# Attention's weights times values: values as the streaming operand from rows of 272 bytes, and first values loaded ahead of the second queries

## The chip, the cores and the metric

The kernel runs on one core of one Trainium2 chip. The metric is the device time of one execution in microseconds (us). Three runs of the kernel before took 785.93, 788.27 and 789.87 us, median 788.27. Engine names: PE is TensorE, DVE is VectorE, ACT is ScalarE, POOL is GpSimd, SP is the engine whose queue issues nearly all transfers.

## The reference

`x` has shape (4, 512, 512), 2048 tokens of 512 features. Attention here is across heads within a token: every token has 32 heads of 16 features, and its 32x32 scores compare its own heads.

```python
q = (x @ wq.T + bq).reshape(B, S, 32, 16)      # k and v alike
scores = einsum('bshd,bstd->bsht', q, k) / sqrt(16)
context = einsum('bsht,bstd->bshd', softmax(scores), v).reshape(B, S, 512)
x = layernorm(x + context)
dq1, dq2, dq3 = nf4_quant_dequant(w1), ...     # 15 comparisons per element, blocks of 64
h = silu(x @ dq1.T) * (x @ dq2.T)              # 1376 hidden features
x = layernorm(x + h @ dq3.T)
```

## The kernel before

The program is written engine by engine, each with its own order of instructions, joined by semaphores. It has three stages.

**Projections.** 48 steps (`tau`), 12 for each of 4 blocks of 512 tokens, make queries, keys and values. They are stored to `qk_parts` and `v_blocks` in HBM and loaded back in the layout of the attention.

**Attention.** It works on 8 half blocks of 256 tokens (`hb`). A half block holds 4 sets `q` of 64 tokens, and 4 groups. So there are 32 groups `G`, each of 16 positions times 4 sets, that is 64 tokens. In each group:

- `scores` (PE): 64 matmuls of 32x32 into `ps_s`.
- `highest`, `shift` (DVE): the row maximum and its subtraction, `prob`; `exp` (ACT); `swap` (DVE): a 32x32 block transpose into `probT`, done one group later.
- `values` (PE), two groups later: for each of the 16 positions the values `v_bd[:, :, position]` are the stationary operand and `probT` the streaming one. `v_bd` is block diagonal over the four sets, 128 partitions by 68 columns (4 sets of 16 features and a column of ones) by 64 positions. Columns of one position stand 64 floats, 256 bytes, apart. The result in `ps_p` has 68 partitions and 32 columns a position.
- `context` (ACT): copies the group's 68x512 from PSUM to `ctx`, three groups later.

After 8 groups (a block of 512 tokens) five `ct` turns transpose `ctx` back to tokens and `add_context` (DVE) divides by the sum and adds to `part`; then `moments`, `norm_1` (ACT, 4 instructions), and four `xt` turns transpose the normalised tokens for the FFN. For the first three blocks this happens inside the groups of the next block: `ct` in groups 8b+10 to 8b+12, moments in 8b+12, norm in 8b+13, `xt` in 8b+14 and 8b+15.

**FFN.** 44 steps of gate, up and down matmuls.

Between all this runs the quantisation of the weights: 15 levels for each of 28 units, one `steep` on ACT and one `lift` on DVE for a level (`nf_y`, `nf_acc`). `LV_A` says how many levels a group takes: 2, and 1 in the `ct` groups. In a group of 2, ACT does in this order: an old group's `context`, one `steep`, `exp`, one `steep`. DVE does `highest`, `swap` of the group before, `shift`, `lift`, anything else, `lift`. Each `lift` needs its `steep`; `exp` needs `shift`.

The SP queue loads the queries and keys of half block 0 and the queries of half block 1 during the last projection steps (`FIRST_STACKS`), then the values of half block 0 (`load_v(0)`), then the keys of half block 1.

At the end of attention the PE does the last `xt` turns, eight turns of dequantised weights (`TAIL_1`, `TAIL_2`) around the last `values`, and goes into the FFN with `gate_up(0)`. A turn waits until the bank that it writes has been read by `high` (ACT) and `low` (DVE).

Of the kernel before, what the change touches and what calls it, by code (L numbers as in the profile page):

```python
# [7 lines left out]
F32 = mybir.dt.float32  # L8
# [6 lines left out]
P = 128  # L15
# [19 lines left out]
def layer_kernel(nc, x, wq, bq, wk, bk, wv, bv, w1, w2, w3, out):  # L35
# [19 lines left out]


# [38 lines left out]

    def turns_of(u):

        kind, g, _ = UNITS[u]
        return [("f", u, s) for s in range(2 if kind == "w" else -(-len(GROUPS[g]) // 2))]
# [14 lines left out]
    def parts_of(u):  # L114
# [6 lines left out]
    NQK, NV, NPV = 5, 4, 4  # L121
# [13 lines left out]
    FIRST_STACKS = {FIRST_LOAD + at: which for at, which in ((0, (0, 0)), (2, (0, 1)), (4, (0, 2)),  # L135
                                                             (6, (1, 0)), (7, (1, 1)), (8, (1, 2)))}
# [27 lines left out]
    CT_AT, XT_AT, MOMENTS_AT, NORM_AT, F_AT = {}, {}, {}, {}, {}  # L164
    for b in range(NBK - 1):
        for k in range(len(HEADS)):
            CT_AT.setdefault(8 * b + 10 + k // 2, []).append(("ct", b, k))
        MOMENTS_AT[8 * b + 12] = b
        NORM_AT[8 * b + 13] = b
        for c in range(KC):  # L170
            XT_AT.setdefault(8 * b + 14 + c // 2, []).append(("xt", b, c))

    LATE = {8 * b + 8 + k: 8 * b + 13 for b in range(NBK - 1) for k in range(2)}
    CONTEXT_AT = {}
    for G in range(GG):
        CONTEXT_AT.setdefault(max(G + 3, LATE.get(G, 0)), []).append(G)
    for G in range(GG):
# [56 lines left out]
    with ExitStack() as both, ExitStack() as proj, ExitStack() as att:  # L234
# [44 lines left out]
        v_bd_0 = sb("v_bd_0", [P, MV, TI], F32, att)  # L279
# [6 lines left out]
        v_bd_1 = sb("v_bd_1", [P, MV, TI], F32, att)  # L286
        x1_st = sb("x1_st", [P, 2, 2, BK], F32R, att)
        v_bd = (v_bd_0, v_bd_1)
# [13 lines left out]
        f3_hb = sb("f3_hb", [P, NJG, E], F32R)  # L302
        minus_i = sb("minus_i", [P, P], F32R)
# [38 lines left out]
        s_pv = sem("s_pv")  # L342
        s_ctx = sem("s_ctx")
# [106 lines left out]
        def turn_shape(key):  # L450
# [8 lines left out]
            js = GROUPS[g][2 * s:2 * s + 2]  # L459
            rows, n = rows_of(js[-1]), len(js)  # L460
            src = src.rearrange("h (j r p) -> h j r p", j=2, r=2)[0:rows, 0:n]
            dst = [t[0:rows, 2 * s:2 * s + n, TB * k:TB * k + TB].rearrange("h j (p r) -> h j r p", r=2)
# [11 lines left out]
        def _(sp):  # L474
# [67 lines left out]
            def load_v(hb):  # L542
                for q in range(Q4):
                    sp.dma_start(v_bd[hb % 2][32 * q:32 * q + 32, DV * q:DV * q + D],
# [819 lines left out]
```

## Time and profile before

| quantity | value |
|---|---|
| median of three runs | 788.27 us |
| the profiled execution | 788.01 us, its span 786.2 us |
| PE busy | 732.7 us (93%) |
| DVE busy | 633.4 us (81%) |
| ACT busy | 484.6 us (62%) |
| attention (first scores to first gate matmul) | 167 to 380 us |
| weights times values, L1043 | 1024 instructions, 125.7 us busy |
| scores, L1030 | 2048 instructions, 44.5 us busy |
| mean granted clock of PE | 0.862 |

The 1.8 us between the span and the execution's time lie outside the instructions. A float32 matmul is two instructions, so 16 positions make 32 rows of L1043; a transpose is one. Matmuls overlap in the pipeline: the spacing of two starts, not the duration of a row, is what one costs.

### The profile page before, as it was taken

What the parts mean: (1) busy time and instruction counts of PE and PEld (TensorE: products, weight loads), DVE (VectorE), ACT (ScalarE), POOL (GpSimd) and SP (SyncE); (2) the same over time, 40 slices, a digit from 0 to 9 for tenths busy, and PEclk for the clock granted to TensorE, in tenths of its full rate; (3) what the DMA queues carried; (4) which work ended last, traced back from release to release, by engine and by line L of the source; (5) the groups of instructions that cost most, each with busy time, mean ns of one, the idle gap of its engine ahead of it and who ended that gap; (6) DMA issues with size and microseconds to landing.
All of it is one profiled execution on the core that took longest, in us unless ns stands there. A gap on an engine that the chain in (4) does not pass through costs nothing.

```text
span 786.2 us, 14305 instructions
## 1 busy us (share of the span) xinstructions
PE 732.7 (93%) x5688; PEld 625.5 (80%) x5688; DVE 633.4 (81%) x876; ACT 484.6 (62%) x650; POOL 106.8 (14%) x101
## 2 busy tenths in 40 slices
PE   4899999966999989999999999999999999999983
PEld 4778788856999989999888877887887788888761
DVE  2699999975888988988888899999977986554386
ACT  3588979773645636546853878877756775333134
POOL 2011012113101101111101121121201111000022
PEclk9999999995555655555799999999999999999995
DMA  9964455999797695995413371211514010330347
GB/s 219 223 182 146 134 166 167 250 305 271 166 261 189 184 283 134 269 216 202 163 26 122 120 230 54 81 39 31 173 59 155 1 61 21 134 119 13 121 147 160
DMA packets 89474, 117.89 MB, mean 150 GB/s; under 512 B 24768, under 2 KB 70848, under 8 KB 86496
## 3 DMA queue, kind: packets, MB, share of 16 engines
q1 hardware_dynamic: 88272, 114.88, 51.6%
q10 hardware_dynamic: 1136, 2.10, 1.2%
q8 instruction: 45, 0.74, 0.4%
q14 instruction: 21, 0.17, 0.1%
HBM read 76.42 MB, written 38.86 MB: 147 GB/s over the span
## 4 chain that ended last, share of the span: by engine, by line
PE 54%; DVE 18%; issue 11%; ACT 8%; DMA 4%; SPq 4%; POOL 1%; DVEq 0%; POOLq 0%; ACTq 0%
PE ps_p L1043 10%; DVE nf_acc L1166 8%; PE ps_s L947 7%; PE ps_s L945 7%; PE ps_s L946 7%; PE ps_p L945 5%; PE ps_p L947 5%; PE ps_p L946 5%; ACT nf_y L777 4%; PE ps_s L1030 3%; PE ps_t L968 2%; DMA qk_parts<-qk_p 2%; DVE part L1298 2%; DMA k_st<-qk_parts 1%; ACT part L852 1%
## 5 line engine op out<-in xcount | busy, mean ns | idle before, releaser
L1166 DVE SCALAR_TENSOR_TENSOR nf_acc<-nf_y,nf_acc 128x1024 f32<-128x1024 f32 (+4 forms) x266 | 298.5, 1122 | 37.6 <-ACT nf_y L777 28.3
L777 ACT ACTIVATE nf_y<-nf_w,bound_b 128x1024 f32<-128x1024 f32 (+4 forms) x285 | 288.9, 1047 | 9.7 <-DVE nf_acc L1162 3.4
L1043 PE MATMUL ps_p<-probT,v_bd 128*68 128x32 f32 x1024 | 125.7, 301 | 7.9 <-issue 7.9
L1043 PEld LDWEIGHTS ps_p<-probT,v_bd 128*68 128x68 f32 x1024 | 122.7, 211 | 9.4 <-issue 8.0
L945 PE MATMUL ps_p<-x_hl,w_hl 128*128 128x512 f32 x192 | 77.6, 404 | 6.1 <-DVE w_hl L1184 4.1
L695 POOL TENSOR_TENSOR nf_w<-nf_w,nf_rec 128x1024 f32<-128x1024 f32 (+4 forms) x19 | 39.5, 2080 | 320.1 <-DVE nf_rec L1150 320.1
L1325 DVE TENSOR_TENSOR silu<-silu,ps_s 128x512 f32<-128x512 f32 (+1 forms) x44 | 30.1, 684 | 61.5 <-PE ps_s L947 61.5
L927 ACT ACTIVATE hid_hl<-silu 128x512 fp32r<-128x512 f32 (+1 forms) x44 | 27.8, 632 | 77.6 <-DVE silu L1325 77.6
L947 PE MATMUL ps_p<-x_hl,w_hl 128*128 128x512 f32 x192 | 75.5, 393 | 0.0
L945 PE MATMUL ps_s<-x_hl,f_ha 128*128 128x512 f32 x192 | 75.4, 393 | 0.0
L946 PE MATMUL ps_p<-x_hl,w_hl 128*128 128x512 f32 x192 | 75.3, 392 | 0.0
L947 PE MATMUL ps_s<-x_hl,f_la 128*128 128x512 f32 x192 | 75.1, 391 | 0.0
L946 PE MATMUL ps_s<-x_hl,f_ha 128*128 128x512 f32 x192 | 75.0, 391 | 0.0
L834 ACT ACTIVATE prob<-prob 128x512 f32<-128x512 f32 x32 | 20.4, 638 | 86.4 <-DVE prob L1209 86.4
L922 ACT ACTIVATE silu<-ps_s 128x512 f32<-128x512 f32 (+1 forms) x44 | 26.2, 595 | 66.1 <-PE ps_s L947 66.0
L702 POOL TENSOR_TENSOR nf_acc<-nf_acc,nf_max 128x1024 f32<-128x1024 f32 (+4 forms) x19 | 37.6, 1977 | 209.7 <-DVE nf_acc L1166 209.6
L947 PE MATMUL ps_s<-x_hl,f_lb 128*128 128x512 f32 (+1 forms) x160 | 62.4, 390 | 0.0
L945 PE MATMUL ps_s<-x_hl,f_hb 128*128 128x512 f32 (+1 forms) x160 | 62.4, 390 | 0.0
L946 PE MATMUL ps_s<-x_hl,f_hb 128*128 128x512 f32 (+1 forms) x160 | 62.3, 390 | 0.0
L1030 PE MATMUL ps_s<-k_st,q_st 128*32 128x32 bf16 x2048 | 44.5, 249 | 9.0 <-issue 6.9
L1030 PEld LDWEIGHTS ps_s<-k_st,q_st 128*32 128x32 bf16 x2048 | 40.0, 171 | 13.5 <-issue 11.5
L945 PEld LDWEIGHTS ps_p<-x_hl,w_hl 128*128 128x128 f32 x192 | 36.5, 190 | 14.7 <-issue 5.4
(110 smaller groups left out, 1253.1 us busy)
## 6 DMA issues: line engine op xcount, KB each, us to landing
x_hl<-x_parts SPq DMA_DIRECT2D x10, 2048.0 KB, 8.5
qk_parts<-qk_p SPq DMA_DIRECT2D x64, 204.0 KB, 2.6
q_st<-qk_parts SPq DMA_DIRECT2D x48, 272.0 KB, 6.8
k_st<-qk_parts SPq DMA_DIRECT2D x48, 272.0 KB, 7.2
x_parts<-x_st SPq DMA_DIRECT2D x16, 512.0 KB, 4.4
nf_w<-in_L_ffn_w SPq DMA_DIRECT2D x24, 256.0 KB, 3.0
dequantised<-nf_acc SPq DMA_DIRECT2D x10, 512.0 KB, 2.6
v_blocks<-v_t SPq DMA_DIRECT2D x16, 256.0 KB, 3.5
```

The costliest lines, as they stand in the source:

```text
L695: pool.tensor_tensor(v, v, nf_rec[0:p, 0:w // QBLOCK].unsqueeze(2).to_broadcast([p, w // QBLOCK, QBLOCK]), ALU.mult).then_inc(s_nnorm, 1)
L702: pool.tensor_tensor(acc, acc, nf_max[0:p, u % 2, 0:w // QBLOCK].unsqueeze(2).to_broadcast([p, w // QBLOCK, QBLOCK]), ALU.mult).then_inc(s ...
L777: act.activation(nf_y[0:p, at % NY, 0:w], nf_w[0:p, u % 2, 0:w], ACT.Identity, bias=bound_b[0:p, i:i + 1], scale=STEEP).then_inc(s_ny, 1)
L922: act.activation(silu[0:rows, s % 2], ps_s[0:rows, 0], ACT.Silu).then_inc(s_silu, 1)
L927: act.activation(hid_hl[0:rows, s % 2, 0], silu[0:rows, s % 2], ACT.Copy).then_inc(s_hh, 1)
L945: pe.matmul(dst, wh, rh, start=start, stop=False)
L946: pe.matmul(dst, wh, rl, start=False, stop=False)
L947: return pe.matmul(dst, wl, rh, start=False, stop=stop)
L1030: t = pe.matmul(ps_s[32 * q:32 * q + 32, G % 2, i * H:(i + 1) * H], q_st[:, :, s], k_st[:, :, s], start=True, stop=True)
L1043: t = pe.matmul(ps_p[0:MV, (G + 3) % NPV, i * H:(i + 1) * H], v_bd[hb % 2][:, :, g * GI + i], probT[:, G % 2, i], start=True, stop=True)
L1166: dve.scalar_tensor_tensor(out=acc, in0=y, scalar=float(NF4[i + 1]), in1=acc, op0=ALU.min, op1=ALU.max).then_inc(s_nacc, 1)
L1325: dve.tensor_tensor(h, h, ps_s[0:rows, 1], ALU.mult).then_inc(s_hid, 1)
```

## The change

`v_bd` gets rows of 68 floats (272 bytes) in place of 64. In `values` the operands trade places: `probT` (32 columns) is stationary and the 68 columns of the values stream; the four positions of a set of four write to different quarters of the PSUM partitions. The result stands transposed to what `context` reads, so two steps are new: `evacuate` (ACT) copies 128x272 from PSUM to `ctmp`, and `back` (PE) transposes it in four pieces into the layout that `context` read before. `ps_p`, four banks, is split into two for each.

The stages after it move by a group: `context` from G+3 to G+4, the `ct` turns, moments, norm and `xt` turns each one group later, so that the last two `xt` turns of the third block stand behind the last group. `LV_A` moves with them. `pairs` writes the list of pairs of tiles in another way. The values of half block 0 are loaded at step 47, ahead of all queries of half block 1.

```diff
+    VS = TI + 4
-    NQK, NV, NPV = 5, 4, 4
+    NQK, NV, NCT = 5, 4, 3
-    FIRST_STACKS = {... (0, (0, 0)), (2, (0, 1)), (4, (0, 2)), (6, (1, 0)), (7, (1, 1)), (8, (1, 2)))}
+    FIRST_STACKS = {FIRST_LOAD: 0, FIRST_LOAD + 2: 1, FIRST_LOAD + 4: 2}
+    FIRST_VALUES = 3 * KC * NBK - 1
-        LV_A[8 * b + 10:8 * b + 13] = [1, 1, 1]
+        LV_A[8 * b + 11:8 * b + 14] = [1, 1, 1]
...
+    LATE = {8 * b + 8 + k: 8 * b + 14 + k // 2 for b in range(NBK - 1) for k in range(4)}
+        CONTEXT_AT.setdefault(max(G + 4, LATE.get(G, 0)), []).append(G)
+        BACK_AT.setdefault(G + 4 if G % 8 == 2 and G > 8 else G + 3, []).append(G)
...
-        v_bd_0 = sb("v_bd_0", [P, MV, TI], F32, att)
+        v_bd_0 = sb("v_bd_0", [P, MV, VS], F32, att)
+        ctmp = sb("ctmp", [P, NCT, 4 * MV], F32, att)
...
+                if tau == FIRST_VALUES:
+                    values_stored(sp, KC)
+                    sp.wait_ge(s_vzero[0], 2 * Q4)
+                    load_v(0)
+            load_stacks(sp, 1, sides=[0])
...
+            def evacuate(G):
+                act.wait_ge(s_pv, G + 1)
+                wait(act, s_back, G - NCT + 1)
+                act.activation(ctmp[:, G % NCT], ps_p[:, G % 2, 0:4 * MV], ACT.Copy).then_inc(s_evac, 1)
...
             for G in range(GG):
+                steep(LV_A[G] // 2)
                 for at in CONTEXT_AT.get(G, []):
                     context(at)
-                steep(LV_A[G] // 2)
                 exp(G)
+                if G >= 2:
+                    evacuate(G - 2)
...
-                    t = pe.matmul(ps_p[0:MV, (G + 3) % NPV, i * H:(i + 1) * H], v_bd[hb % 2][:, :, g * GI + i],
-                                  probT[:, G % 2, i], start=True, stop=True)
+                    a, j = divmod(i, 4)
+                    t = pe.matmul(ps_p[32 * j:32 * j + 32, G % 2, a * MV:(a + 1) * MV], probT[:, G % 2, i],
+                                  v_bd[hb % 2][:, :, g * GI + i], start=True, stop=True)
...
+            def back(G):
+                pe.wait_ge(s_evac, G + 1)
+                wait(pe, s_ctx, G - 1)
+                for a in range(4):
+                    t = pe.transpose(ps_p[0:MV, 2 + G % 2, P * a:P * a + P], ctmp[:, G % NCT, a * MV:(a + 1) * MV],
+                                     ident[:])
```

On ACT, in ordinary groups of the attention (`prob` is `exp`, `nf_y` is `steep`, `ctx` is `context`), before:

```order
L834 ACTIVATE prob<-prob 128x512
L777 ACTIVATE nf_y<-nf_w,bound_b 128x1088
L844 ACTIVATE ctx<-ps_p 68x32x16
L777 ACTIVATE nf_y<-nf_w,bound_b 128x1088
L834 ACTIVATE prob<-prob 128x512
L777 ACTIVATE nf_y<-nf_w,bound_b 128x1088
L844 ACTIVATE ctx<-ps_p 68x32x16
```

and after:

```order
L872 ACTIVATE ctx<-ps_p 68x32x16
L855 ACTIVATE prob<-prob 128x512
L863 ACTIVATE ctmp<-ps_p 128x272
L798 ACTIVATE nf_y<-nf_w,bound_b 128x1088 x2
L872 ACTIVATE ctx<-ps_p 68x32x16
L855 ACTIVATE prob<-prob 128x512
```

The copy to `ctmp` now stands between `exp` and the pair of `steep` whose first belongs to this group; `context` has gone to the place ahead of `exp`.

On SP, around the first loads of values (`v_bd`), before:

```order
L430 DMA q_st<-qk_parts 16x8704 x2
L588 DMA qk_parts<-qk_p 128x3x272 x2
L430 DMA q_st<-qk_parts 16x8704 x2
L594 DMA v_blocks<-v_t 128x2x256
L430 DMA q_st<-qk_parts 16x8704 x2
L594 DMA v_blocks<-v_t 128x2x256 x3
L544 DMA v_bd<-v_blocks 32x16x64 x4
L540 DMA k_st<-q_st 32x8704
L430 DMA k_st<-qk_parts 16x8704 x6
```

and after:

```order
L610 DMA qk_parts<-qk_p 128x3x272 x6
L616 DMA v_blocks<-v_t 128x2x256 x3
L561 DMA v_bd<-v_blocks 32x16x64 x4
L616 DMA v_blocks<-v_t 128x2x256
L447 DMA q_st<-qk_parts 16x8704 x6
L557 DMA k_st<-q_st 32x8704
L447 DMA k_st<-qk_parts 16x8704 x6
```

The six transfers of queries of half block 1 went behind the values; those of its keys (`k_st`, x6) still come last.

On PE, from the last group's scores to the first gate matmul (`part` are `xt` turns, `f_la` weight turns), before:

```order
L1030 MATMUL ps_s<-k_st,q_st 32x32 x64
L1043 MATMUL ps_p<-probT,v_bd 68x32 x16
L972 MATMUL ps_t<-ident,part 128x128 x8
L1043 MATMUL ps_p<-probT,v_bd 68x32 x16
L982 MATMUL ps_t<-ident,f_la 128x128 x8
L989 MATMUL ps_s<-ident,f_la 128x128 x8
L1043 MATMUL ps_p<-probT,v_bd 68x32 x16
L989 MATMUL ps_s<-ident,f_la 128x128 x8
L982 MATMUL ps_t<-ident,f_la 128x128 x8
L945 MATMUL ps_s<-x_hl,f_ha 128x512
```

and after:

```order
L1063 MATMUL ps_s<-k_st,q_st 32x32 x64
L1078 MATMUL ps_p<-v_bd,probT 32x68 x16
L1087 MATMUL ps_p<-ident,ctmp 68x128 x4
L1005 MATMUL ps_t<-ident,part 128x128 x8
L1078 MATMUL ps_p<-v_bd,probT 32x68 x16
L1005 MATMUL ps_t<-ident,part 128x128 x8
L1015 MATMUL ps_t<-ident,f_la 128x128 x8
L1022 MATMUL ps_s<-ident,f_la 128x128 x8
L1087 MATMUL ps_p<-ident,ctmp 68x128 x4
L1078 MATMUL ps_p<-v_bd,probT 32x68 x16
L1022 MATMUL ps_s<-ident,f_la 128x128 x8
L1015 MATMUL ps_t<-ident,f_la 128x128 x8
L1087 MATMUL ps_p<-ident,ctmp 68x128 x4
L978 MATMUL ps_s<-x_hl,f_ha 128x512
```

The same three `values` stand there in both. New behind the last scores are three `back`, and a second pair of `xt` turns (8 transposes), which stood ahead of those scores before.

## Rows read from the trace of the kernel before

**Rows 1.** the page, part 2: granted clock over 40 slices of 19.7 us

```profile
PEclk9999999995555655555799999999999999999995
```

**Rows 2.** timeline of PE: start us, us, engine, line, tiles, count

```profile
193.46 1.34 PE L1030 MATMUL ps_s<-k_st,q_st 128*32 128x32 bf16 x64
194.74 3.95 PE L1043 MATMUL ps_p<-probT,v_bd 128*68 128x32 f32 x32
255.47 1.95 PE L972 MATMUL ps_t<-ident,part 128*128 128x128 f32 x8
```

**Rows 3.** windows of PE: us, busy (count), granted clock, DMA share, GB/s

```profile
254.00:255.00 1.00, 1.00 (x11) 0.50 0.25 34
260.00:261.00 1.00, 1.00 (x11) 1.00 0.00 0
```

**Rows 4.** chain that ended last: start us, us, what

```profile
392.78 0.87 PE ps_t L982 x8
```

**Rows 5.** timeline of DVE, attention groups 5 to 7

```profile
201.03 0.63 DVE L1205 TENSOR_REDUCE smax<-ps_s 128x16 f32<-128x512 f32 x1
205.90 0.68 DVE L1205 TENSOR_REDUCE smax<-ps_s 128x16 f32<-128x512 f32 x1
209.59 1.30 DVE L1166 SCALAR_TENSOR_TENSOR nf_acc<-nf_y,nf_acc 128x1088 f32<-128x1088 f32 x1 [0.61 <-ACT nf_y L777]
211.07 0.69 DVE L1205 TENSOR_REDUCE smax<-ps_s 128x16 f32<-128x512 f32 x1 [0.19 <-PE ps_s L1030]
```

**Rows 6.** timeline of ACT, group 6

```profile
207.82 0.63 ACT L834 ACTIVATE prob<-prob 128x512 f32<-128x512 f32 x1 [1.59 <-DVE prob L1209]
208.35 1.20 ACT L777 ACTIVATE nf_y<-nf_w,bound_b 128x1088 f32<-128x1088 f32 x1
```

**Rows 7.** groups of ACT, shapes apart: count, busy us, mean ns, idle before

```profile
L803 ACT ACTIVATE f_hb<-ps_t 128x384 fp32r<-128x384 f32 x2 | 0.9, 478 | 0.0
L803 ACT ACTIVATE f_hb<-ps_t 96x256 fp32r<-96x256 f32 x2 | 0.8, 381 | 0.0
```

**Rows 8.** chain that ended last, group 2

```profile
175.15 7.91 issue
```

**Rows 9.** timeline of the SP queue: issue of transfers

```profile
171.76 6.63 SPq L544 DMA_DIRECT2D v_bd<-v_blocks  x4
179.42 4.10 SPq L430 DMA_DIRECT2D k_st<-qk_parts  x6
```

**Rows 10.** transfers issued at 150 to 200 us: count, KB, us to landing

```profile
k_st<-qk_parts SPq DMA_DIRECT2D x14, 272.0 KB, 6.3
```

**Rows 11.** timeline of DVE: group starts (smax), one block maximum

```profile
189.67 0.69 DVE L1205 TENSOR_REDUCE smax<-ps_s 128x16 f32<-128x512 f32 x1 [7.36 <-PE ps_s L1030]
195.75 0.68 DVE L1205 TENSOR_REDUCE smax<-ps_s 128x16 f32<-128x512 f32 x1
248.18 1.21 DVE L1138 TENSOR_REDUCE nf_max<-nf_w 128x16 f32<-128x1024 f32 x1
249.31 0.68 DVE L1205 TENSOR_REDUCE smax<-ps_s 128x16 f32<-128x512 f32 x1
257.17 0.63 DVE L1205 TENSOR_REDUCE smax<-ps_s 128x16 f32<-128x512 f32 x1
262.96 0.68 DVE L1205 TENSOR_REDUCE smax<-ps_s 128x16 f32<-128x512 f32 x1
285.02 0.69 DVE L1205 TENSOR_REDUCE smax<-ps_s 128x16 f32<-128x512 f32 x1
291.75 0.69 DVE L1205 TENSOR_REDUCE smax<-ps_s 128x16 f32<-128x512 f32 x1 [0.59 <-PE ps_s L1030]
298.77 0.68 DVE L1205 TENSOR_REDUCE smax<-ps_s 128x16 f32<-128x512 f32 x1
364.40 0.68 DVE L1205 TENSOR_REDUCE smax<-ps_s 128x16 f32<-128x512 f32 x1
```

**Rows 12.** timeline of PE: first gate matmul

```profile
379.95 0.78 PE L945 MATMUL ps_s<-x_hl,f_ha 128*128 128x512 f32 x1
```

More of the change, by code:

```diff
@@ L94, in layer_kernel, with pairs @@
     NU0 = len(GROUPS[0]) + 2
+    def pairs(g):
+        js, out = list(GROUPS[g]), []
+        while js:
+            n = 2 if len(js) > 1 and rows_of(js[1]) == P else 1
+            out.append(js[:n])
+            js = js[n:]
+        return out
     def turns_of(u):
         kind, g, _ = UNITS[u]
-        return [("f", u, s) for s in range(2 if kind == "w" else -(-len(GROUPS[g]) // 2))]
+        return [("f", u, s) for s in range(2 if kind == "w" else len(pairs(g)))]
     def valid(g):
@@ L458, in turn_shape @@
                 return src, [t[:, s, :, jj * P:jj * P + rows] for t in f1[g % 2]]
-            js = GROUPS[g][2 * s:2 * s + 2]
-            rows, n = rows_of(js[-1]), len(js)
+            js = pairs(g)[s]
+            rows, n, at = rows_of(js[0]), len(js), js[0] - GROUPS[g][0]
             src = src.rearrange("h (j r p) -> h j r p", j=2, r=2)[0:rows, 0:n]
-            dst = [t[0:rows, 2 * s:2 * s + n, TB * k:TB * k + TB].rearrange("h j (p r) -> h j r p", r=2)
+            dst = [t[0:rows, at:at + n, TB * k:TB * k + TB].rearrange("h j (p r) -> h j r p", r=2)
                    for t in f3[g % 2]]
@@ L637, in _ @@
                 for key in XT_AT.get(G, []):
[L638 to L640 removed]
+                    store_x1(key)
+            for key in XT_AT.get(GG, []):
+                store_x1(key)
             def store_out(n, q):
@@ L903, in _ @@
                 steep(LV_A[G] - LV_A[G] // 2)
+            context(GG - 4)
+            evacuate(GG - 2)
+            for key in XT_AT.get(GG, []) + TAIL_1:
+                high(key)
             context(GG - 3)
-            for key in TAIL_1:
-                high(key)
-            context(GG - 2)
             steep(LV_T[0])
@@ L910, in _ @@
                 high(key)
-            context(GG - 1)
+            evacuate(GG - 1)
+            context(GG - 2)
             steep(LV_T[1])
@@ L922, in _ @@
                 act.activation(silu[0:rows, s % 2], ps_s[0:rows, 0], ACT.Silu).then_inc(s_silu, 1)
+                if s == 0:
+                    context(GG - 1)
                 steep(LV_F[s][0])
@@ L1104, in _ @@
                 scores(G)
+                if G >= 2:
+                    values(G - 2)
                 for key in CT_AT.get(G, []):
                     turn(key)
-                if G >= 2:
-                    values(G - 2)
+                for at in BACK_AT.get(G, []):
+                    back(at)
                 for key in XT_AT.get(G, []):
@@ L1111, in _ @@
             values(GG - 2)
-            for key in TAIL_1:
+            for key in XT_AT.get(GG, []) + TAIL_1:
                 turn(key)
+            back(GG - 3)
             values(GG - 1)
@@ L1116, in _ @@
                 turn(key)
+            back(GG - 2)
             pe.wait_ge(s_minus_i, 1)
@@ L1120, in _ @@
                 gate_up(s)
+                if s == 0:
+                    back(GG - 1)
                 for key in F_TURNS.get(s, []):
@@ L1285, in _ @@
             swap(GG - 1)
-            for key in TAIL_1:
+            for key in XT_AT.get(GG, []) + TAIL_1:
                 low(key)
```

55 lines of the change are left out of this document (26 added, 29 removed).

## The prediction

> **What bounds the kernel now.** I read the page first. PE is busy 93% of the span, but its granted clock stands at half in the slices of the attention [rows 1], and the FFN behind it runs at full clock without gaps. So whatever the attention gives back moves the FFN forward, and the question is what paces a group there. The timeline of PE shows scores (1.3 us) and weights times values (3.9 us) back to back [rows 2]: 5.2 us. The timeline of DVE shows how near the next bound is. Where PE does not hold it, one group's row maximum follows the last by 4.87 us (201.03 to 205.90). Two groups later it takes 5.2 us or so, with 0.19 us of waiting for PE [rows 5]. Those 4.87 us are a ring through two engines: maximum, transpose and subtraction on DVE (1.9 us), `exp` on ACT (0.53 us to the next start), one `steep` behind it (1.2 us), and the `lift` that waits for it, shown by the 0.61 us of idle ahead of it (1.2 us) [rows 5, 6]. So PE can give at most 0.3 us in an ordinary group before this ring decides.
>
> The second place is the start: PE stands 7.91 us ahead of the first weights times values [rows 8], while the loads of its values are still being issued [rows 9]. The maximum of group 3 then waits 7.36 us [rows 11].
>
> **Weights times values.** Its spacing is 3.9/32 = 0.121 us an instruction, and it does not follow the clock: the same eleven instructions touch one microsecond at clock 0.50 and at 1.00 [rows 3]. A transpose with 128 contiguous columns as weights and 128 streaming does follow it: 1.88/8 = 0.23 us at half (start of the row to the start of what follows; I take 0.22) and 0.87/8 = 0.11 us at full [rows 2, 4]. So the old price is that of loading 68 weight columns from rows 256 bytes apart, and that goes away. The new price is streaming: 68/128 of a transpose, 0.117 us at half clock, 0.058 us at full. The trace shows no float32 matmul into a quarter of the partitions, so I bound it. Below: the pace of the scores, which also write quarters, 1.34/64 = 0.021 us, times 32 = 0.7 us [rows 2]. Above: no overlap and the old strided pace, 3.9 us. Between them: the two passes of one matmul follow each other, but the second overlaps the first of the next quarter, 16 x 0.117 = 1.9 us at half clock, 0.9 us at full. I take 1.9 us.
>
> The Trainium skill speaks against this choice in "Advanced Engine Details and Errata", section Memory Cachelines: consecutive reads that each hit another 16-byte line pay a penalty, and at least two hits on a line are needed. 272-byte rows give every streamed column its own line. By that rule the sum is that of the third rival below. The trace agrees for the weights at 256 bytes; no row shows a float32 stream.
>
> **`back`** adds four transposes a group, 4 x 0.22 = 0.9 us at half clock, 0.45 us at full. PE per ordinary group: 1.3 + 1.9 + 0.9 = 4.1 us at half clock, under the ring. In a `ct` group the turns come on top, and that is about 5.9 us against 6.1 us of DVE work (below). PE no longer bounds either.
>
> **`evacuate`** is what joins the ring: it stands between `exp` and the `steep` that the next `lift` waits for. No ACT row has 272 columns. 384 take 0.478 us and 256 take 0.381 us [rows 7], so 272 take about 0.40 us. ACT starts the next instruction some 0.1 us before a row ends (0.63 us against 0.53 us in [rows 6]): 0.29 us. Bounds are 0.25 and 0.40 us. Its waits are old by then: `values` of two groups before is ready when `swap` is, some 6 us earlier. `context` moves ahead of `exp`, where ACT was idle 1.59 us [rows 6] in a group where it had done its share before; it stays hidden, also where two stand together. The ring becomes 4.87 + 0.29 = 5.16 us. That is what PE made it before. In an ordinary group the gain is nil.
>
> **Group 4 to group 31.** Before: 364.40 - 195.75 = 168.65 us [rows 11], 27 groups. After:
> - 11 ordinary groups at 5.16: 56.8.
> - 9 `ct` groups, DVE-bound, `evacuate` hidden under its additions: twice 6.73 - 0.59 = 6.14 (285.02 to 291.75 less the wait for PE), then 298.77 - 291.75 = 7.02; three times 19.3 = 57.9.
> - 3 norm groups: 257.17 - 249.31 = 7.86, plus 0.29, so 24.5. Here four normalising instructions stand in the same ring.
> - 4 `xt` groups: 262.96 - 257.17 = 5.79, plus 0.29, so 24.3.
> - three block maxima that fall in groups costed without one, about 1.25 each [rows 11]: 3.8.
>
> Sum 167.3 us, a gain of 1.4. The bounds of `evacuate` (18 groups) move it by -0.7 and +2. PE's waits in `ct` groups are what is gained, the ring takes most of it back.
>
> **The start.** Six transfers of queries and one store of values no longer stand ahead of the first values. Six such transfers take 4.1 us to issue [rows 9], the store 0.6 us by that pace. So the values come about 4.5 us sooner, weights times values of group 0 starts at 178.5 and ends at 180.4. ACT's `evacuate(0)` must wait for that, and its `steep` behind it; with 0.3 + 1.2 + 1.2 group 3 starts near 183.1 in place of 189.67. What is late next is group 4's scores: they need the keys of half block 1, and the same transfers stand ahead of their last issue as before (183.52 from [rows 9]); with 6.3 us to landing [rows 10] and 1.3 us of scores this is 191.2, say 191.5, in place of 195.75: 4.2 us gained. If those land earlier it is 6, if the values wait on bandwidth rather than on the queue it is 2.
>
> **The end.** Before, from the last group's maximum to the first gate matmul: 379.95 - 364.40 = 15.55 us [rows 11, 12], PE busy throughout. After, PE has two `values` (3.8), a pair of `xt` turns (1.8), eight weight turns (7.0) and two `back` (1.8) at half clock, 14.4 us. But it can't start before `swap(30)` (1.2 us), and it waits twice: the second `xt` pair for `low` of the first in the same bank (1.0 us), the first weight turn for `low` of the second pair, which DVE does only behind the last `swap` (1.7 us). That is 18.3 us, 2.7 more than before. At full clock PE's part halves, the chain through ACT (8 `high`, 2 `steep`) decides, and it is about 14.6 us, 0.9 less. The clock here stood at half before; I take 2.0 more, near that.
>
> Nothing of the FFN changes but one `back` (0.4 us) and a `context` that `down(0)` waits for, both ahead of it by a whole gate and up. The wider `v_bd` clears and `pairs` cost nothing: POOL waits in that place. Sum: -4.2 - 1.4 + 2.0 = -3.6 us on the profiled 788.01; the median shown, 788.27, is 0.3 above that, so 784.6 us.
>
> **Rivals.**
> - *The clock rises.* PE streams more of the time than before. Then the end costs -0.9 in place of +2.0, and the `ct` groups keep their distance from PE. With 5 us of start this is -5 - 1.4 - 0.9 = -7.3: 781. For it: full clock came back in the attention for some microseconds after `xt` transposes [rows 3]. Against: PE will be idle a fifth of each group.
> - *Given back.* The keys of half block 1 or code loading use up the start (gain 1.5 us), and the end costs its 2.7: -0.2, so 788.
> - *Slower: the stream is strided and quarters don't overlap.* Then weights times values stays at 3.9 us and `back` comes on top: 6.1 us of PE in an ordinary group against 5.2, 0.9 us in each of 11 ordinary and 9 `ct` groups (18 us), three `back` and the waits at the end (5 us), less 4 us of start: +19, 807 us. It decides from about 3.0 us a group, where PE passes the ring (5.16 - 1.3 - 0.9); at 3.2 us the gain is used up. For it: the strided weights of rows 3. Against: the scores read both operands from rows of 544 bytes and pass at 0.021 us.
>
> The Trainium skill, "TensorEngine Tiling (Array Packing)", Performance Considerations, advises just this swap with column tiling for up to four times; with an estimate of a quarter of 16 x 2 x 0.117 it would be 0.9 us at half clock. The sum would be better only at the end, by 2 us.
>
> **Chances.** Forecast 0.50 (own range 781.5 to 788), higher clock 0.22, given back 0.14, slower 0.14. This kernel's measurement can tell about 0.5% from no change (3.9 us: below 784.3, above 792.2). Faster: half of the forecast's share, nearly, and the higher clock, 0.46. Same: the rest of the forecast and the given-back case, 0.38. Slower 0.16. The range goes from 779 to 796 us: it takes in the first three and the mild part of the fourth.
>
> **What would show it.** Weights times values: 32 rows in about 1.9 us at clock 0.5, 0.9 us at 1.0. Ordinary groups: maxima 5.1 to 5.2 us apart, the idle ahead of the second `lift` up from 0.6 to 0.9 us and released by `nf_y`, no wait for PE. Group 3 near 183, group 4 near 191.5 with its scores released by a transfer. `ct` groups without waits for PE. Last maximum to first gate matmul 14.6 to 18.3 us. I am wrong if PE releases the maxima again, if ordinary groups fall under 5 us, or if the FFN's length changes.

## The result, and the profile after

The changed kernel took 800.14 us (median of four runs, 796.66 to 802.20) against 787.1 us for the kernel before beside it: a ratio of 1.016, 95% interval 1.0135 to 1.0185. The prediction said 784.6 and a range to 796. It is 13 us slower and outside the range. The profiled execution is the fastest of the four: 796.66 us, its span 794.9 us, where that of before had 786.2. Its projections happened to end 1.95 us sooner than those of before (group 0's maximum at 166.63 and 168.58 us), so the loss behind them is 10.7 us in this pair. The stages below account for that; the rest of the 13 us lies in the slower executions, which have no trace.

The page, part 2 (40 slices of 19.9 us: PE's busy tenths, its granted clock, the DMA engines), answers to [rows 1]:

```profile
PE   4899999963665574764899999999999999999982
PEclk9999999986878766776899999999999999999995
DMA  9964455999799796691413253201424010430347
```

PE is busy 58% of the attention now (166.6 to 387.4 us) at a mean granted clock of 0.74, where it was busy 91% (168.6 to 380 us) at 0.54. Next the new price of weights times values, from the page (part 5), against 125.7 us for the same 1024 in the kernel before:

```profile
L1078 PE MATMUL ps_p<-v_bd,probT 128*32 128x68 f32 x1024 | 40.5, 304 | 30.3 <-issue 22.2
```

Rows of an ordinary group, three engines by start time, answer to [rows 2, 5, 6, 7]:

```profile
222.18 0.68 DVE L1255 TENSOR_REDUCE smax<-ps_s 128x16 f32<-128x512 f32 x1
224.09 0.63 ACT L855 ACTIVATE prob<-prob 128x512 f32<-128x512 f32 x1 [1.56 <-DVE prob L1259]
224.62 0.38 ACT L863 ACTIVATE ctmp<-ps_p 128x272 f32<-128x272 f32 x1
224.90 2.34 ACT L798 ACTIVATE nf_y<-nf_w,bound_b 128x1088 f32<-128x1088 f32 x2
225.06 1.06 PE L1087 MATMUL ps_p<-ident,ctmp 128*68 128x128 f32 x4 [0.29 <-ACT ctmp L863]
226.05 1.36 PE L1063 MATMUL ps_s<-k_st,q_st 128*32 128x32 bf16 x64
226.12 1.29 DVE L1216 SCALAR_TENSOR_TENSOR nf_acc<-nf_y,nf_acc 128x1088 f32<-128x1088 f32 x1 [0.88 <-ACT nf_y L798]
227.34 0.68 DVE L1255 TENSOR_REDUCE smax<-ps_s 128x16 f32<-128x512 f32 x1
```

That is the forecast, row by row: maxima 5.16 us apart, `evacuate` 0.38 us and 0.28 us to the next start, the idle ahead of the second `lift` 0.88 us and released by `nf_y`, no wait for PE. What was not in the forecast is on PE's own timeline, in groups 4 to 7:

```profile
196.78 0.45 PE L1078 MATMUL ps_p<-v_bd,probT 128*32 128x68 f32 x7 [3.79 <-issue]
202.58 1.05 PE L1063 MATMUL ps_s<-k_st,q_st 128*32 128x32 bf16 x48 [1.12 <-issue]
205.12 0.99 PE L1063 MATMUL ps_s<-k_st,q_st 128*32 128x32 bf16 x43
211.14 0.62 PE L1063 MATMUL ps_s<-k_st,q_st 128*32 128x32 bf16 x21 [5.03 <-issue]
```

The counts are what to read: 43 of the 64 scores of a group, then 5 us of nothing, then the other 21. No semaphore stands in there, all operands are in place. From 192 to 366 us there are eleven such stops of 0.2 us or more inside a `scores` or a `values`, 20.8 us in all; in the kernel before there are four, 2.3 us in all. Ahead of 192 us both kernels have two, and the kernel before showed one of them as long as the new ones, in the scores of group 2 (PE of before):

```profile
174.31 0.84 PE L1030 MATMUL ps_s<-k_st,q_st 128*32 128x32 bf16 x33 [3.49 <-issue]
```

And on ACT a wait that was 0.2 us before (the view of waits, 165 to 400 us: us in total, times, longest):

```profile
ACT x_st L824 <- DMA x_parts<-x_st: 6.6, 6, 2.5
```

The stages, from the starts of the `smax` rows (group 0, 4, 31) and the first gate matmul, as [rows 11, 12] have them for before:

| run (profiled execution) | group 0 to 4 | 4 to 31 | 31 to gate | gate to end | 31 to end |
|---|---|---|---|---|---|
| before | 27.17 | 168.65 | 15.55 | 406.25 | 421.80 |
| changed | 27.09 | 175.13 | 18.59 | 407.46 | 426.05 |
| predicted change | -4.2 | -1.4 | +2.0 | 0 | +2.0 |
| measured change | -0.1 | +6.5 | +3.0 | +1.2 | +4.2 |

The last column is the safe one: over all runs "gate to end" lies between 405.4 and 407.5 us in either form, and it trades with "31 to gate" (e3: 20.26 and 405.74 us, the same sum as the changed kernel).

### The profile page after: what moved, and what is told of

Same layout as the page of the kernel before. It is cut to its first block, busy times and chain, and to the rows that moved or that the text cites. A ratio compares the mean times of both kernels' runs of the same rounds, so it can differ in the third digit from the quotient of the medians.

```text
span 794.9 us, 14656 instructions
## 1 busy us (share of the span) xinstructions
PE 666.4 (84%) x5816; PEld 543.3 (68%) x5816; DVE 633.5 (80%) x876; ACT 493.2 (62%) x682; POOL 107.3 (13%) x101
## 4 chain that ended last, share of the span: by engine, by line
PE 45%; DVE 23%; issue 13%; ACT 8%; DMA 6%; SPq 3%; POOL 1%; DVEq 0%; POOLq 0%; ACTq 0%
DVE nf_acc L1216 8%; PE ps_p L978 7%; PE ps_s L978 7%; PE ps_s L980 7%; PE ps_s L979 7%; PE ps_p L980 7%; PE ps_p L979 7%; ACT nf_y L798 4%; DMA x_parts<-x_st 2%; DVE part L1348 2%; DVE prob L1259 2%; DMA qk_parts<-qk_p 2%; DVE smax L1255 2%; ACT part L880 1%; DVE st L1287 1%
## 5 line engine op out<-in xcount | busy, mean ns | idle before, releaser
L1078 PE MATMUL ps_p<-v_bd,probT 128*32 128x68 f32 x1024 | 40.5, 304 | 30.3 <-issue 22.2
L1078 PEld LDWEIGHTS ps_p<-v_bd,probT 128*32 128x32 f32 x1024 | 31.2, 139 | 33.5 <-issue 26.9
L1087 PE MATMUL ps_p<-ident,ctmp 128*68 128x128 f32 x128 | 27.9, 366 | 23.5 <-ACT ctx L872 22.3
```

The lines of the kernel that those rows point to most:

```text
L1078: t = pe.matmul(ps_p[32 * j:32 * j + 32, G % 2, a * MV:(a + 1) * MV], probT[:, G % 2, i], v_bd[hb % 2][:, :, g * GI + i], start=True, stop ...
L1087: t = pe.transpose(ps_p[0:MV, 2 + G % 2, P * a:P * a + P], ctmp[:, G % NCT, a * MV:(a + 1) * MV], ident[:])
```

## The experiments

Unless said otherwise a ratio is to the kernel before, with its 95% interval. That kernel's median was 787.45 to 787.97 us in every set. The step of group n is the time from its row maximum to that of the next.

**e1, rows of 272 bytes alone.** The kernel before, values still stationary:

```diff
+    VS = TI + 4
...
-        v_bd_0 = sb("v_bd_0", [P, MV, TI], F32, att)
+        v_bd_0 = sb("v_bd_0", [P, MV, VS], F32, att)
...
```

`v_bd_1` has the same edit, and the loads write the first 64 columns of each row.

> The kernel before with one thing changed: rows of v_bd are 272 bytes in place of 256; the values stay the stationary operand, no new steps. Theory A (the 0.121 us of one weights-times-values instruction is the cost of weight columns 256 bytes apart, and the distance of 256 bytes itself is what is slow): the 32 rows take about 2 us in place of 3.9, PE falls under the ring of DVE and ACT, ordinary groups come 4.87 us apart in place of 5.17, the ct groups lose their waits for PE: 6 to 9 us faster in all. Theory B (any weight column on a line of its own costs this, as the rule of 16-byte lines says, or float32 weights load at this pace at any distance): still 3.9 us, the time stays within 2 us.

792.04 us, ratio 1.0054 [1.0029, 1.0080]. A group's weights times values took 4.25 us instead of 3.95:

```profile
214.30 4.25 PE L1045 MATMUL ps_p<-probT,v_bd 128*68 128x32 f32 x32
```

Theory B on the mechanism: loading spaced weights isn't dear because of the distance of 256 bytes; 272 is no cheaper. The whole was 4.1 us slower, where B said within 2. Padding pays only with the values streaming.

**e8, streaming without the padding.** The changed kernel with `VS = TI`.

> The changed kernel with rows of v_bd of 64 floats (256 bytes) in place of 68: the streamed columns lie 256 bytes apart. Theory A (what cost 3.95 us a group before was loading weights from spaced rows; a stream of 68 columns does not care for their distance, 256 or 272 bytes): 32 rows in 1.15 to 1.25 us, the whole within 1 us of 800. Theory B (the padding is what makes the stream fast): 32 rows take 2 us or more, ordinary groups lengthen from 3.0 us up, 803 us or more.

834.85 us, ratio 1.061 [1.057, 1.0645]: Theory B, and far beyond it. The 32 rows took 2.0 us instead of 1.2, and the neighbours paid too. In one group DVE's subtraction runs beside the stream, in the next the `lift` does (DVE and PE of e8):

```profile
205.52 2.06 DVE L1259 TENSOR_TENSOR prob<-ps_s,smax 128x512 f32<-128x512 f32 x1
205.71 2.05 PE L1078 MATMUL ps_p<-v_bd,probT 128*32 128x68 f32 x32
...
212.10 0.65 DVE L1259 TENSOR_TENSOR prob<-ps_s,smax 128x512 f32<-128x512 f32 x1
212.67 2.85 DVE L1216 SCALAR_TENSOR_TENSOR nf_acc<-nf_y,nf_acc 128x1088 f32<-128x1088 f32 x1
213.35 2.00 PE L1078 MATMUL ps_p<-v_bd,probT 128*32 128x68 f32 x32
```

The same subtraction takes 2.06 us while PE streams columns 256 bytes apart and 0.65 us while it doesn't; then the `lift` is the one that is long, 2.85 us against 1.29. With 272 bytes DVE's rows keep their length. The group grows from 5.2 to 6.6 us, 31 us from group 4 to 31. The Trainium skill's rule ("Advanced Engine Details and Errata", Memory Cachelines: at least two hits on a 16-byte line are needed, else there is a penalty) would fit the run at 256 bytes, 0.063 us an instruction, but not the one at 272, 0.037, though both give every column its own line.

**e2, the loads alone.** The kernel before with the first values ahead of the second queries (the `FIRST_STACKS` and `FIRST_VALUES` lines of the change).

> The kernel before with one part of the change alone: the values of half block 0 are loaded at step 47, ahead of the queries of half block 1. Theory A (the gain of the start is real but the transfers behind it bound it): weights times values of group 0 starts at 176 to 178 in place of 183, group 4's maximum comes 1 to 2.5 us earlier than 195.75, since keys and the next NF4 weights land no sooner, and the time falls by 1 to 2 us. Theory B (the reordering is itself what costs in the changed kernel): group 4 no earlier, the time rises by 2 us or more.

788.18 us, ratio 1.0007 [0.9983, 1.0031]. No gain: weights times values of group 0 started at 178.1 us, but group 3 to 4 took 13.2 us; neither theory, A's 1 to 2 us are missing. In the changed kernel the same stands (DVE and PE, two views):

```profile
181.03 0.69 DVE L1255 TENSOR_REDUCE smax<-ps_s 128x16 f32<-128x512 f32 x1 [0.42 <-PE ps_s L1063]
192.52 1.29 DVE L1188 TENSOR_REDUCE nf_max<-nf_w 128x17 f32<-128x1088 f32 x1 [6.24 <-DMA nf_w<-in_L_ffn_w]
193.72 0.68 DVE L1255 TENSOR_REDUCE smax<-ps_s 128x16 f32<-128x512 f32 x1
```

```profile
190.83 1.30 PE L1063 MATMUL ps_s<-k_st,q_st 128*32 128x32 bf16 x62 [7.84 <-DMA k_st<-qk_parts]
```

Group 3 is early, group 4 waits for the same bytes as before. The DMA share from 180 to 204 us is 0.95 to 1.13 in windows of 4 us. That the bytes wait on full engines and not on their issue is argued: the six transfers of these keys were issued from 176.45 to 181.4 us, in the kernel before from 179.42 to 183.5 [rows 9], and the last three took 8.2 us to land.

**e3, stores of tokens first.** In the changed kernel SP issues a group's stores of `x_st` ahead of its loads:

```diff
                 levels(LV_A[G])
+                for key in XT_AT.get(G, []):
+                    store_x1(key)
...
-                for key in XT_AT.get(G, []):
-                    store_x1(key)
```

> The changed kernel with one order changed on SP: in each group the stores of the xt turns are issued ahead of the loads of that group (stacks of queries and keys, values, x1). Theory A (the xt groups lost their time because these stores now stand behind 3.3 MB of stack loads, and the next turns wait for their slot): ACT's waits of 6.6 us for the store vanish, group 16 takes 6.1 in place of 9.5 us, group 24 6.1 in place of 7.4, the end shrinks by 1 to 2 us: 5 to 7 us faster than the changed kernel, that is 793 to 795. Theory B (those waits are covered by code loading or by PE anyway): less than 2 us.

**e4, `evacuate` ahead of `exp`** in the changed kernel:

```diff
+                if G >= 3:
+                    evacuate(G - 2)
                 exp(G)
-                if G >= 2:
-                    evacuate(G - 2)
...
```

> The changed kernel with the copy to ctmp ahead of exp in place of behind it, from group 3 on. Theory A (it stands in the ring through DVE and ACT): ordinary groups 4.87 in place of 5.16 us, norm and xt groups 0.3 us less, in sum 4 to 5 us faster than the changed kernel, 795 to 796. Theory B (something else paces these groups, PE or code loading): groups stay above 5.1 us and the time within 2 us of the changed kernel.

**e5, both of these.**

> The changed kernel with the two earlier edits together: the stores of the normalised tokens ahead of a group's loads, and evacuate ahead of exp. Each alone took 796.7 to 797.0 us against 800.1. Theory A (losses are separate: the ring paid for evacuate, the stores waited for on ACT, the stops of PE with nothing to wait for): the gains add, 793 to 794 us; ordinary groups 4.86 to 4.93 us apart, steps of groups 16 and 24 near 7.0 and 5.9 us, stops of PE unchanged. Theory B (both edits only moved the same loss, the last of several chains decides): 796 to 797 us again.

e3 took 797.04 us, ratio 1.0124 [1.0092, 1.0155], e4 796.69 us, 1.0127 [1.009, 1.0163], e5 793.75 us, 1.0092 [1.0061, 1.0122]. The two gains, 3.1 and 3.4 us, add up to 6.4 (800.14 - 793.75), as separate losses do (e5's Theory A); each alone is less than its Theory A said (5 to 7 and 4 to 5 us), and about as large as the noise of a comparison of two such ratios, so the steps of the groups are the better evidence. The step of group 16 fell from 9.48 to 7.26 us and that of group 24 from 7.39 to 6.10 in e3; ordinary groups from 5.16 to 4.9 us in e4. PE's stops in groups 2, 6 and 7 stayed at the same instructions in all three; of the later ones some went and others came (e3 has one of 3.63 us in the values of group 25 and not the 2.80 us of group 17). The end stayed: group 31 to the end is 425.7 to 426.0 us.

**e6, the tight version.** `evacuate` ahead of `exp`; `back` two groups after the scores, `context` three; so `ct` turns, moments, norm and `xt` turns go back to the groups of the kernel before, and no pair of `xt` turns stands behind the last scores:

```diff
-        CONTEXT_AT.setdefault(max(G + 4, LATE.get(G, 0)), []).append(G)
-        BACK_AT.setdefault(G + 4 if G % 8 == 2 and G > 8 else G + 3, []).append(G)
+        CONTEXT_AT.setdefault(max(G + 3, LATE.get(G, 0)), []).append(G)
+        BACK_AT.setdefault(G + 3 if G % 8 == 2 and G > 8 else G + 2, []).append(G)
...
-            XT_AT.setdefault(8 * b + 15 + c // 2, []).append(("xt", b, c))
+            XT_AT.setdefault(8 * b + 14 + c // 2, []).append(("xt", b, c))
```

> The changed kernel with evacuate ahead of exp, back two groups after the scores instead of three, context three instead of four, and with that ct turns, moments, norm and xt turns in the groups in which they stood before the change. No pair of xt turns is left behind the last group. Theory A (the shift by one group cost the waits for stores on ACT and the longer end; the new form of weights times values is itself cheap): steps of groups 16 and 24 at 6 us or below, last maximum to first gate matmul 14.5 to 15.5 us in place of 18.6, ordinary groups 4.9 us; with PE's stops (some 4 us of waits in groups 4 to 7 and 21) left in, 784 to 787 us against 787 before. Theory B (the shift is harmless, and whatever stops PE grows with the new instructions themselves): 792 us or more, with the stops in other places.

789.16 us, ratio 1.0025 [1.0007, 1.0043], between the two theories, nearer A: 11.0 us of the 13 are gone. Group 31 to the end is 420.9 us, waits for stores 1.2 us. The rest of A's number is missing in groups 10 to 28, where PE's stops had moved to other places but stayed as many (12, 23 us in all).

**e7, little traffic for the values.** The changed kernel; of the values of half blocks 1 to 7 one feature of 16 is loaded.

> The changed kernel, but of the values of half blocks 1 to 7 only one of 16 features is loaded (32 KB in place of 512 KB each, a sixteenth of the packets of 256 bytes); weights times values runs over what stands in v_bd. Only the traffic changes. Theory A (PE stops in the middle of scores and values because its instructions are fetched over transfers that queue behind these loads): the stops of 3.8 us in weights times values of group 2 and 5.0 us in the scores of group 7 fall below 1.5 us each, the ones near later loads of values too (3.0 at group 13, 2.8 and 2.5 at groups 18 and 19); group 4 starts 2 to 5 us sooner; in all 4 to 8 us less than 800. Theory B (the stops come at fixed places of the instruction stream whatever the traffic): same places, 3 to 5 us long, time within 2 us of 800.

801.73 us, ratio 1.0185 [1.0153, 1.0216]: the whole didn't move, as Theory B said, and yet one stop did, which it excluded. The stop in the scores of group 7 is gone, the one in weights times values of group 2 has grown to 6.24 us:

```profile
202.99 0.45 PE L1079 MATMUL ps_p<-v_bd,probT 128*32 128x68 f32 x7 [6.24 <-issue]
...
210.40 1.06 PE L1064 MATMUL ps_s<-k_st,q_st 128*32 128x32 bf16 x48 [2.72 <-issue]
...
213.33 1.57 PE L1064 MATMUL ps_s<-k_st,q_st 128*32 128x32 bf16 x64
```

The last row is group 7: 64 in one piece. With the values out of the way SP had issued the queries and keys of half block 2 right behind (188.7 to 196.2 us); they kept the DMA engines full to 208 us (share 1.02 from 188 us on), over the first stop, and left them nearly empty at the second. The windows (us, busy of five engines, granted clock, DMA share, GB/s) of the stop in the changed kernel, and of the same instructions in e7:

```profile
205.20:207.20 2.00, 0.91 (x43) 0.77 (x43) 2.00 (x4) 0.75 (x2) 0.00 (x0) 1.00 1.07 252
207.20:209.20 2.00, 0.00 (x0) 0.00 (x0) 1.48 (x2) 1.68 (x3) 0.00 (x0) 1.00 0.91 151
209.20:211.10 1.90, 0.00 (x0) 0.00 (x0) 1.29 (x1) 1.89 (x3) 0.00 (x0) 0.77 1.25 155
```

```profile
212.00:214.00 2.00, 2.00 (x60) 1.42 (x54) 2.00 (x4) 0.45 (x2) 0.00 (x0) 0.70 0.00 0
214.00:216.00 2.00, 2.00 (x74) 1.67 (x67) 1.11 (x2) 2.00 (x4) 0.00 (x0) 1.00 0.04 8
```

And the DMA queues of the changed kernel from 207.1 to 209.1 us, in the middle of the stop:

```profile
q1 hardware_dynamic: 695, 0.29, 85.7%
q8 instruction: 1, 0.02, 3.8%
```

One transfer of 16 KB on an instruction queue lands there, among the 256-byte packets of `v_bd`.

The kept traces hold a sharper sign. Count PE's recorded instructions in order, matmuls, weight loads and those of its queue. In all 17 traces together 134 stops of 0.2 us or more stand inside a `scores` or a `values`, and every one of them stands at a count of 192 or 193 plus a multiple of 256. The changed kernel crosses 46 such places and has 46 transfers of 16,384 bytes on queue q8, the kernel before 45 and 45. At each of these stops the transfer of that number ended 1.2 to 1.9 us before PE went on; for the stop of 5.03 us it ran from 208.28 to 209.50 us, and PE went on at 211.14. So the stops are PE waiting for its next block of 256 instructions.

**e9 and e10, little traffic for both forms.** The changed kernel and the kernel before, with of half blocks 2 to 7 a sixteenth of the values and of the queries and keys.

> The changed kernel, but of half blocks 2 to 7 only a sixteenth of the values and of each query or key transfer's 8704 columns only 544 are loaded: some 24 MB of traffic fewer in the attention. Every instruction of PE, ACT and DVE stays. Theory A (the stops of PE inside scores and weights times values are instruction blocks that come late over busy DMA engines; in run e7 the stop of 5.0 us in the scores of group 7 went where the DMA share was 0.14, the one in group 2 stayed where it was 1.0): from group 4 on no stop above 1 us, the waits of ACT for stores of tokens go too, group 4 to 31 takes what the ring gives, 165 to 168 us, last maximum to first gate matmul 15 to 17 us, the whole 788 to 791 us. Theory B (the stops belong to the instruction stream, whatever the traffic): stops of 2.5 to 3.5 us stay at groups 18, 19 and 24, group 4 to 31 at 172 us or more, 796 us or more.

> The kernel before with the same transfers cut short (half blocks 2 to 7). Theory A (in the form before, PE itself paces a group, and its stops of about a microsecond cost little): group 4 to 31 at 166 to 168.7 us, the whole 784 to 788 us, so that with little traffic the two forms lie within 4 us of each other, where they lay 13 apart. Theory B (traffic harms both alike): the kernel before gains as much as the changed one, and the distance stays near 10 us.

e9 took 793.80 us, ratio 1.0079 [1.0056, 1.0102], e10 784.96 us, 0.9963 [0.9943, 0.9982]. Cutting the traffic gave 6.3 us to the changed kernel and 2.9 to the one before. In e9 one stop inside a `scores` or `values` is left after 192 us, in e10 none:

```profile
199.82 0.43 PE L1080 MATMUL ps_p<-v_bd,probT 128*32 128x68 f32 x7 [4.00 <-issue]
```

It stands where the values of half block 1, which are still loaded in full, are on their way (DMA share 1.11 in its first half). It stands at a block's end too: the transfer began at 196.98 us, 1.2 us after PE had run out. Theory A on the stops held but for this one. Its total did not (expected 788 to 791), and what is left is not the traffic of these loads: group 31 to the end is 425.87 us as in the changed kernel, and 8.8 us lie between the two forms, where A of e10 said under 4 (B near 10).

**e11 and e12, loads in another order.** The twelve transfers of queries and keys of a half block, four at a time, in the tight version and in the kernel before.

> The tight version (run e6) with the same loads spread out: of the twelve transfers of queries and keys of a half block, which stood together, four at a time in three groups, and the values one group later. Nothing is left out. Theory A (late instruction blocks are a matter of long bursts): stops of 1 us and more after group 4 become fewer and shorter (12 us of them in e6's attention), group 4 to 31 at 164 to 167 us instead of 169.2, the whole 783 to 787 us, under e6's 789.2 and at or below the kernel before. Theory B (a block meets some transfer anyway): within 1.5 us of e6.

> The kernel before, with only that spreading of the loads. Theory A (its PE is not held up by its instructions, so bursts cost it nothing but the start of group 4): within 1 us of 787.5; if the values of half block 1, a group later now, leave the queue to the keys, up to 2 us less from an earlier group 4. Theory B (spreading helps any form of this kernel by itself): 3 us or more less.

e11 785.81 us, ratio 0.9979 [0.9957, 1.0000]; e12 788.09 us, 1.0009 [0.9990, 1.0029]. The stops in e11 fell from 23 to 14 us and its time is in Theory A's range, but not group 4 to 31: 168.94 us, where A said 164 to 167. e12 is as its Theory A said. But nothing held SP back, and for half block 2 it issued the transfers in a row all the same (194.4 to 204.7 us), with a stop of 4.35 us in front.

**e13, e14, e15, loads held back.** Now each piece waits for its group; in the tight version, the changed kernel and the kernel before:

```diff
+                if g < 2 and 0 < hb < NHB - 1:
+                    sp.wait_ge(s_score, G + 1)
...
+                    load_stacks(sp, hb + 1, [1 + g])
...
```

> The tight version with the loads held back: SP issues the three pieces of a half block's queries and keys (four transfers each) in three successive groups, each after the scores of its group are done, the values in the group behind; the values of half block 1 are issued only with group 4. Nothing is left out. Theory A (PE's stops inside scores and values are late instruction blocks behind queued loads): the stop in weights times values of group 2 (4.4 us in e11) falls under 1.5 us, in all the stops from 192 us on are under 8 us against 14 in e11 and 24 in e6; the keys of half block 1 stand with less in front of them, so that group 4 starts up to 1 us sooner; 781 to 784 us. Theory B (any transfers do it): stops as in e11, 785 to 788 us.

> The changed kernel with the same holding back and nothing else. Theory A: the stops of 3.8 us (group 2), 5.0 us (group 7) and 3.6 us (group 24) fall under 1.5 us, the stores of tokens stand behind four transfers instead of twelve, so steps of groups 16 and 24 fall from 9.5 and 7.4 to 6.5 to 7 us; group 4 to 31 at 167 to 170 us instead of 175; the end stays; 793 to 796 us. Theory B: 799 to 801 us.

> The kernel before with the same holding back. Theory A (PE works without a gap there and an instruction block lasts it longer than it takes to come): group 4 to 31 between 165.7 (run e10) and 168.7 us, the whole 785.5 to 788 us. Theory B (holding back helps by itself, whatever the form): 784 us or less, and then e13 must be compared with this run.

| run | median us | ratio | 0 to 4 | 4 to 31 | 31 to end |
|---|---|---|---|---|---|
| e13 | 783.72 | 0.9951 [0.9939, 0.9963] | 25.71 | 167.45 | 420.90 |
| e14 | 794.09 | 1.0084 [1.0068, 1.0101] | 26.37 | 171.19 | 425.16 |
| e15 | 789.67 | 1.0024 [1.0007, 1.0041] | 27.71 | 169.56 | 421.10 |

e13 beats both kernels: 4.0 us under the kernel before, and 6.0 us under that kernel with the same holding back (e15). Holding back gave 5.4 us to the tight version, 6.0 us to the changed kernel and took 1.9 us from the kernel before, where one stop of 2.71 us now fell into the scores of group 7 (step of group 6: 7.39 us); e15 is outside both of its theories, 1.7 us above A. e13 and e14 lie in the time of their Theory A, e14 not in its stretch from group 4 to 31. The early stops shrank (1.87 and 1.16 us in e13 instead of 4.35 and 3.66 in e11; the first was to fall under 1.5), but my number for the sum was wrong: still 14 us in ten stops, while the groups around them mostly kept their steps. Holding back has a price of its own: in e14 the scores of group 20 waited 5.51 us for keys that came too late, and the step of group 19 rose from 6.05 to 9.03 us:

```profile
291.76 1.35 PE L1071 MATMUL ps_s<-k_st,q_st 128*32 128x32 bf16 x64 [5.51 <-DMA k_st<-qk_parts]
```

The early stops of e13:

```profile
195.69 0.68 PE L1087 MATMUL ps_p<-v_bd,probT 128*32 128x68 f32 x11 [1.87 <-issue]
...
208.18 0.65 PE L1072 MATMUL ps_s<-k_st,q_st 128*32 128x32 bf16 x25 [1.16 <-issue]
```

## Why the prediction was wrong

The loss of 13 us by runs: the place of `evacuate`, the shift by one group and the longer end together 11.0 (changed to e6), the meeting of PE's stops with bursts of loads 5.4 to 6.0 (e6 to e13, changed to e14). That makes 16.4 us from the changed kernel to e13, which lies 4.0 us under the kernel before: that much the new form gives, once both are out of the way. It still has 14 us of stops, so it is what these runs reached and not a bound.

- **Weights times values.** Mechanism right, size too careful: 1.2 us a group at either clock, where I took 1.9 and 0.9. It didn't matter, as the ring decided.
- **The ring.** Right: 5.16 us, `evacuate` 0.28 in it. I wrote that the ring takes the gain back, but not that it needn't: e4 shows 4.9 us with the copy ahead of `exp`.
- **Group 4 to 31**, -1.4 predicted, +6.5 measured. The failed step: the sum took each group at its ring or DVE price (167.3 us) and gave PE no stops, because the kernel before shows hardly any behind 192 us; its one of 3.49 us, at 174.31 us, was a warning that I passed over. With little traffic (e9) the stretch is 169.85 us, of which 2.6 are one stop left (step of group 4: 7.75) and 1.1 a store wait (step of group 16: 7.15 against 6.1); 166.2 without them, against my 167.3. So that sum was sound where the transfers are few, and the 8.9 us to 175.13 are transfers: late instructions on PE, late stores on ACT. How they divide is not shown: the stops and the waits overlap with slack of PE and with each other.
- **The store waits** I missed altogether. I moved the `xt` turns by a group in the sum and did not ask which transfers their stores would then stand behind. In groups 16 and 24 their stores now stand on SP behind twelve loads of 3.3 MB, and `high` of the next turn needs the store of the one before it.
- **The start**, -4.2 predicted, -0.1 measured. The values came early (group 3 at 181.0, predicted 183.1), but my next-late step, scores of group 4 at 191.5, took the landing time of 6.3 us [rows 10] as fixed. Under full engines it was 8 us, and `nf_max`, which stands ahead of that maximum on DVE, waited for weights that took 10.5 us. The clause "if the values wait on bandwidth rather than on the queue it is 2" named the cause and still gave 2 us; e2 shows 0.2 (26.99 us from group 0 to 4, and 27.17 before).
- **The end**, +2.0 predicted, +4.2 with the FFN's part. PE did wait for `low` of both `xt` pairs, 0.94 and 2.89 us (worked out: 1.0 and 1.7), but the second pair's `high` also waited 1.58 and 0.81 us for the stores of the first:

```profile
376.08 0.60 ACT L824 ACTIVATE x_st<-ps_t 128x512 fp32r<-128x512 f32 x1 [1.58 <-DMA x_parts<-x_st]
377.45 1.11 PE L1015 MATMUL ps_t<-ident,f_la 128*128 128x128 f32 x4 [2.89 <-DVE x_st L1234]
387.44 0.52 PE L978 MATMUL ps_s<-x_hl,f_ha 128*128 128x512 f32 x1 [2.20 <-DVE f_la L1234]
```

  and after the last wait (2.20 us, for a `low` of the weights, which the sum lacks) the FFN began at half clock: eight matmuls 0.43 us apart against three in the kernel before, 0.23 us apart later. That is about 1.0 us by an estimate from these spacings, and I had put it at nothing. Every run with that pair behind the last scores has 425.2 to 427.6 us from group 31 to the end, every run without it 418.5 to 422.6.
- **The rivals.** "The clock rises" came true in its condition (0.74 against 0.54 in the attention) and not in its gain: the groups were not held by PE's pace, and the end cost +4.2 where that rival had -0.9. "Given back" named code loading in passing; it is the nearest, and was priced from a trace in which PE's work covered it. The slower rival had the wrong mechanism: quarters do overlap, and 272-byte rows stream well.

What is shown and what is argued. Shown: PE's stops stand where a block of 256 instructions ends, with the block's transfer landing just before PE goes on (all 17 traces), and they come and go with the DMA share at unchanged instructions (e7, e9, e10). The Trainium skill ("Runtime: NRT & Kernel Launch", Instruction fetch mechanics) says that an engine's sequencer fetches its instructions over a DMA queue of its own, in blocks of 16 KiB, while it runs the block before; the trace agrees on the size (16,384 bytes). Its sentence that crossing a block is mostly hidden fits the kernel before behind 192 us (2.3 us of stops), not the changed kernel (20.8).

Why the kernel before hardly has them: two things can be read between 192 and 366 us, how long PE had from entering a block to its last instruction, and how late the transfer of the next block began after PE entered.

| run | shortest stay in a block | stays under 5 us | median start of the transfer | stops |
|---|---|---|---|---|
| before | 5.9 us | 0 of 22 | 1.9 us | 4, 2.3 us |
| changed | 3.5 us | 8 of 23 | 3.2 us | 11, 20.8 us |
| e10, before with little traffic | 5.9 us | 0 of 22 | 0.5 us | none |
| e9, changed with little traffic | 3.5 us | 7 of 23 | 0.8 us | 1, 4.0 us |

The new form runs through some blocks in little more than half the time, and under traffic the next block's transfer starts late. e8, whose slower stream leaves one stay under 5 us, has 5 stops and 9.2 us. That the short stays are what makes the difference is argued from these numbers; no run changed them alone. Open stay why a transfer starts late (5.7 us and more after the block was entered at seven of the eleven stops, 12.9 at the first), in which order the queues are served, and why the transfers start later in the changed kernel than in the kernel before at nearly the same DMA share (0.83 and 0.85 of the attention).

## What to carry to other kernels

Before an engine is made faster, look at what its slowness covered: here PE's long instructions hid the arrival of its own next instructions and the bursts of loads beside them, and a gain clear of the noise came only when the loads were held to the pace of the groups. When a stage moves by one step, list the transfers it issues and what stands ahead of them on their queue; here a store of 0.5 MB behind 3.3 MB of loads, and two turns behind the last group, cost more than the new matmuls gave (e6 against e4: 7.5 us, and 4.0). Loads that are held back must still come in time (e14, group 20). A stride is judged by the run on both sides: 272 bytes was better than 256 for the stream (1.2 against 2.0 us), worse for the weights (4.25 against 3.95).

## What the runs showed of the hardware

- Streaming 68 float32 columns from rows of 272 bytes into a quarter of the partitions costs 0.037 us an instruction (two a position), at half and at full clock alike (changed kernel, start to next start: 1.15 us for 32 at 199.28 us and clock 0.50, 1.12 us at 203.44 us and 1.00); from rows of 256 bytes 0.063 us (e8).
- During the 256-byte stream instructions of other engines take longer: a 128x512 subtraction on DVE from 0.65 to 2.06 us, a `lift` from 1.29 to 2.85.
- PE can stop for up to 6.2 us (e7) between two instructions of one kind with no semaphore, at the end of a block of 256 instructions; it went on 1.2 to 1.9 us after a transfer of 16,384 bytes on its instruction queue had landed. With little traffic the transfers are hardly noticed (e10: no stop from 192 to 366 us).
